# Batch 0's split q and k go to DRAM in two portions from two queues, and maxima units run 7 ahead in place of 8

## The reference

```
x = x + attention(modulate(x, cond))     # 16 heads of 8, rotary, causal softmax, output projection
x = x + ffn(experts(x, cond))            # 2 shared + 8 routed experts (top 2), then 8 zones (top 3)
```

## Time and profile before

| | us |
|---|---|
| median of 3 runs (lowest to highest) | 197.34 (197.03 to 198.95) |
| the profiled execution | 197.56 |
| its span | 195.8 |
| around the span | 1.76 |

### The profile page before, as it was taken

One profiled execution on the slowest core, in us unless ns is written; L12 is line 12 of the kernel. 1 busy time (PEld: TensorE's weight loads), 2 busy tenths in 40 slices (PEclk: granted clock), 3 DMA queues, 4 the chain that ended last, 5 costly groups with the idle time before them and its releaser, 6 DMA issues.

```text
span 195.8 us, 3320 instructions
## 1 busy us (share of the span) xinstructions
PE 180.1 (92%) x1006; PEld 124.1 (63%) x1006; DVE 143.7 (73%) x459; ACT 137.9 (70%) x228; POOL 83.6 (43%) x97
## 2 busy tenths in 40 slices
PE   7897698999999999898999999999799989999992
PEld 3654364666656666664467685786467857788881
DVE  5589699889898989896167974679969657556642
ACT  4479255486867768698843874576778899899880
POOL 4517359343324546464620620202467950497000
PEclk9999999999999999999999999999999999999999
DMA  4927657767585769431110899000000000001001
GB/s 143 363 85 229 203 189 233 205 176 223 161 264 157 223 184 253 141 96 54 54 50 5 274 310 311 5 2 0 0 2 3 0 0 0 0 2 57 0 0 54
DMA packets 13985, 23.06 MB, mean 118 GB/s; under 512 B 2632, under 2 KB 3784, under 8 KB 13912
## 3 DMA queue, kind: packets, MB, share of 16 engines
q1 hardware_dynamic: 13392, 22.46, 37.1%
q10 hardware_dynamic: 576, 0.39, 0.6%
HBM read 17.42 MB, written 6.09 MB: 120 GB/s over the span
## 4 chain that ended last, share of the span: by engine, by line
PE 61%; DVE 15%; ACT 11%; issue 6%; DMA 3%; SPq 2%; POOL 1%; DVEq 0%; ACTq 0%; POOLq 0%
PE psum L1414 9%; PE psum L1291 8%; PE psum L1416 8%; PE psum L1415 8%; PE psum L1342 7%; PE psum L1322 5%; DVE psum L680 3%; DMA t_q_pad<-scratch 2%; PE psum L1235 2%; PE psum L1249 2%; PE psum L1181 2%; DVE t_raw L826 2%; PE psum L1325 2%; ACT t_q_pad L1044 1%; DVE t_raw L830 1%
## 5 line engine op out<-in xcount | busy, mean ns | idle before, releaser
L680 DVE CUSTOM_DVE_ANT_0 psum<-psum,t_causal 128x128 f32<-128x128 f32 (+3 forms) x128 | 59.3, 525 | 8.0 <-PE psum L1291 7.3
L992 ACT ACTIVATE t_probs<-psum 128x768 f32<-128x768 f32 (+1 forms) x48 | 41.0, 880 | 4.9 <-PE psum L1322 3.3
L1291 PE MATMUL psum<-t_stacked,t_q_pad 128*128 128x256 f32 (+2 forms) x128 | 37.3, 361 | 3.9 <-issue 1.7
L576 POOL TENSOR_SCALAR_AFFINE_SELECT t_probs<-t_probs 128x512 f32<-128x512 f32 x32 | 20.0, 636 | 31.6 <-ACT t_probs L992 28.4
L1291 PEld LDWEIGHTS psum<-t_stacked,t_q_pad 128*128 128x128 f32 x128 | 21.4, 188 | 18.8 <-DVE t_row_max L680 10.8
L844 DVE SCALAR_TENSOR_TENSOR t_q_pad<-psum,t_zw_all,t_q_pad 128x512 fp32r<-128x512 f32 x24 | 17.9, 749 | 11.7 <-ACT t_q_pad L1042 11.6
L1028 ACT ACTIVATE t_raw<-psum 128x512 f32<-128x512 f32 x24 | 14.3, 595 | 10.4 <-PE psum L1460 7.7
L1342 PE MATMUL psum<-t_probs,t_v_all 128*32 128x512 f32 (+3 forms) x256 | 20.5, 439 | 0.0
L612 POOL TENSOR_TENSOR t_q_pad<-t_raw,t_q_pad 128x512 fp32r<-128x512 f32 x8 | 10.3, 1288 | 20.1 <-ACT t_q_pad L1044 20.1
L1322 PE MATMUL psum<-t_q_mov,t_k_pad 128*128 128x512 f32 (+1 forms) x64 | 18.4, 373 | 0.2
L680 DVE DVE_READ_ACCUMULATOR2_ANT t_row_max<- 128x1 f32 x128 | 18.4, 144 | 0.0
(11 more groups left out here) (228 smaller groups left out, 389.8 us busy)
## 6 DMA issues: line engine op xcount, KB each, us to landing
t_stacked<-scratch SPq DMA_DIRECT2D x14, 256.0 KB, 3.6
t_probs<-in_L_ffn_Wa SPq DMA_DIRECT2D x2, 1024.0 KB, 8.3
t_q_pad<-scratch SPq DMA_DIRECT2D x28, 64.0 KB, 3.2
t_k_pad<-scratch SPq DMA_DIRECT2D x28, 64.0 KB, 2.2
scratch<-t_o_sb SPq DMA_DIRECT2D x7, 256.0 KB, 2.0
t_raw<-in_experts SPq DMA_DIRECT2D x7, 256.0 KB, 3.4
scratch<-t_dn_hi SPq DMA_DIRECT2D x4, 256.0 KB
scratch<-in_rest SPq DMA_DIRECT2D x2, 448.0 KB
```

Of the source, the lines that this page charges most:

```text
L576: last = G.affine_select(out=tri, in_=tri, compare_op=ALU.is_ge, fill=0.0, base=0, pattern=[[0, HG], [1, P]], channel_multiplier=-1)
L680: last = V.tensor_tensor_reduce(scores, scores, causal[:, S - width:S], 1.0, 3 * BIG, ALU.add, ALU.max, row_max[s][:, qb, j:j + 1])
L992: A.activation(probs[s][:, c, 2 * h2:2 * h2 + 2, 0:w], ST[:, slot_of("exp", n, u):slot_of("exp", n, u) + 2, 0:w], ACT.Exp, scale=float(1.0 ...
L1291: last = T.matmul(ring("max", n, u)[:, i * 2 * P:i * 2 * P + width], q_pad[s][:, j, qb * P:(qb + 1) * P], stacked[:, 2 * n + 1, 0:width], ...
```

## The change

Four edits, which come together:

1. `spill` takes a queue, a range of groups, and the semaphores to count on. Batch 0 is written in two portions: group 1's 32 rows (64 KB for each DMA) and groups 2 and 3's 64 rows (128 KB).
2. The first portion of q and k stays where the spill was, on SP. Of the second portion, q goes on SP behind `pad_k(0)`, and k on ScalarE's own queue, between `copy_v(0)` and `copy_projection(1)`.
3. `ld_stack[n]` becomes a pair: M(n,0) waits for k's stack alone, the lay step for q's. The list of SP is reordered to match; the two parameter loads go behind `pad_k(1)`.
4. LEAD is 7: stage 0 holds 16 units (still 12 before the lay step), and in the stages n >= 1 each M unit sits one place later: places 0 to 4 are M(n+1,7..11), 5 to 11 are M(n+2,0..6).

```diff
-LEAD, FIRST = 8, 3
+LEAD, FIRST = 7, 3
...
+        spilled_1 = [sem(f"spilled_1{x}") for x in "qk"]
         spilled = [sem(f"spilled_{x}") for x in "qk"]
-        ld_stack = {n: sem(f"ld_stack{n}") for n in range(BY_PE, GROUPS)}
+        ld_stack = {n: [sem(f"ld_stack{x}{n}") for x in "qk"] for n in range(BY_PE, GROUPS)}
...
+        def spill(queue, first, last, i, done):
+
+            b = first // NG
+            q = slice(32 * (first - b * NG), 32 * (last - b * NG))
+            blocks = laid_blocks(first, last, i)
+            queue.wait_ge(hi_ready, 4 * b + (i + 1 if b else 3 + i))
+            for r in ((1, 2), (1, 3))[i]:
+                queue.dma_start(blocks[r], f32_of(qk_hi[q, i, :])).then_inc(done[i], 16)
+            queue.wait_ge(lo_ready, 4 * b + (i + 1 if b else 3 + i))
+            queue.dma_start(blocks[(3, 2)[i]], f32_of(qk_lo[q, i, :])).then_inc(done[i], 16)
...
             spill_rest()
-            spill(0, 0)
-            spill(0, 1)
+            spill(sp, 1, 2, 0, spilled_1)
+            spill(sp, 1, 2, 1, spilled_1)
             sp.wait_ge(rest_rows, 16 * 2)
-            sp.wait_ge(spilled[0], 16 * SPILLS)
+            sp.wait_ge(spilled_1[0], 16 * SPILLS)
             sp.wait_ge(pad1_zero, 1)
             pad_q(1)
-            sp.wait_ge(spilled[1], 16 * SPILLS)
-            load_stacked(1)
+            sp.wait_ge(spilled_1[1], 16 * SPILLS)
+            load_stacked_part(1, 1)
             sp.wait_ge(pads_zero, 1)
             pad_k(0)
-            load_stacked(2)
+            spill(sp, 2, NG, 0, spilled)
+            load_stacked_part(1, 0)
+            sp.wait_ge(spilled[1], 16 * SPILLS)
+            load_stacked_part(2, 1)
+            sp.wait_ge(spilled[0], 16 * SPILLS)
             pad_q(2)
+            load_stacked_part(2, 0)
+            sp.wait_ge(pads_zero, 2)
+            pad_k(1)
             sp.dma_start(small[:], io["small"]).then_inc(ld_small, 16)
             sp.dma_start(gate_rows[:], io["sel_e"]).then_inc(ld_sele, 16)
-            sp.wait_ge(pads_zero, 2)
-            pad_k(1)
...
             copy_v(0)
+            spill(act, 2, NG, 1, spilled)
             copy_projection(1)
...
                     pe.wait_ge(q_padded[s], 16 * HG * ((n + 1) // 2))
-                    pe.wait_ge(ld_stack[n], 16 * 2)
+                    pe.wait_ge(ld_stack[n][1], 16)
...
                     pe.wait_ge(rep_copied, 4)
+                else:
+                    pe.wait_ge(ld_stack[n][0], 16)
                 bank = ring("lay", n)
```

More of the change, by code:

```diff
@@ L354, in laid, with laid_blocks @@
             return scratch[GROUPS + 1 + i * (GROUPS - BY_PE) + n - BY_PE]
[L356 to L360, removed]
+        def laid_blocks(first, last, i):
+            at = GROUPS + 1 + i * (GROUPS - BY_PE) - BY_PE
+            return scratch[at + first:at + last].rearrange("g (j r d) t -> r (g j) d t", j=HG, r=KB)
+        def spill(queue, first, last, i, done):
[7 more added lines that the diff above has]
+            queue.dma_start(blocks[(3, 2)[i]], f32_of(qk_lo[q, i, :])).then_inc(done[i], 16)
         def slot_of(*item):
@@ L403, in pad_k @@
                     sp.dma_start(f32_of(k_pad[s][q, j, :]), src).then_inc(k_padded[s], 16)
[L405 to L412, removed]
             def spill_rest():
                 for i in range(2):
-                    first = GROUPS + 1 + i * (GROUPS - BY_PE)
-                    slots = scratch[first:first + GROUPS - BY_PE]
-                    rows = slots.rearrange("g (j r d) t -> r (g j) d t", j=HG, r=KB)[0]
+                    rows = laid_blocks(BY_PE, GROUPS, i)[0]
                     sp.dma_start(rows, io["rest"][i].unsqueeze(0).broadcast_to(
@@ L428, in load_stacked_part @@
             def load_stacked_part(n, i):
-                sp.dma_start(f32_of(stacked[:, 2 * n + i, :]), laid(n, i)).then_inc(ld_stack[n], 16)
+                sp.dma_start(f32_of(stacked[:, 2 * n + i, :]), laid(n, i)).then_inc(ld_stack[n][i], 16)
             def store_sums(n):
@@ L494, in _ @@
                 if n == 0:
-                    spill(1, 0)
+                    spill(sp, NG, GROUPS, 0, spilled)
                 if n + 2 < GROUPS:
@@ L498, in _ @@
                 if n == 0:
-                    spill(1, 1)
+                    spill(sp, NG, GROUPS, 1, spilled)
                 if n == NG:
```

## The result

| | before | after |
|---|---|---|
| median, us (lowest to highest, 20 runs each) | 197.41 (196.81 to 199.84) | 196.27 (195.28 to 198.88) |
| ratio, 95% interval | | 0.9922 (0.9897 to 0.9947) |
| profiled execution | 197.56 | 195.3 |
| its span | 195.8 | 193.5 |

The change saves 0.8%: clear of no change, but within the 1% that the prediction took for its limit. The forecast was 194.5, a gain of 3.1 us; the medians show 1.14. Single executions of one kernel differ by several us, and all ratios leave out those more than 1.5% above the kernel's fastest. The profiled execution of after is the second quickest of its 20, so the profiles show 2.26 us.

A forecast was written before the change was run, and what follows sets the result against it. The prediction took TensorE's 1.71 us hole before M(1,0), ended by a landing, then VectorE, then TensorE with small waits as the bound. It summed 197.56 - 1.5 (stage 0) - 1.6 (LEAD) to 194.5, range 193.2 to 196.9.

The forecast's parts named there:

- Waiting for k's stack alone: Ahead of M(1,0): without any other edit TensorE could start at 22.9, so 1.2 us are gained.
- T = 19.3: The time SP issues k's stack of group 1, taken between bounds of 17.6 and 20.3.
- project(1) as the new start: k's stack lands at 21.9, so TensorE goes on when project(1) ends at 22.47; the whole 1.71 us is gained.
- T stays at 20.3: First rival: the first portion lands no sooner, SP issues group 1's k stack at 20.3; 195.4 with LEAD, chance 0.15.
- pad_k(0)* follows: In stage 0 k_pad[0] lands at 23.8, before E(0,0) wants it at 24.33: nothing late.
- (at T = 20.3: 0.4): If SP issues k's stack of group 1 at 20.3, pad_k(0) is 0.4 us late for E(0,0).
- The signs of being wrong: M(1,0) starting after 23.5, group 1's lay step after 34, or lay steps 3 to 4 not below 8.97 - 0.1 apart.
- q_pad(2): Queued on SP behind q's second portion, it is issued near 27 and lands at 31.3; M(2,0) waits 1.7 us.
- The charge of 0.2: Stage 0: q_pad(2) puts group 1's lay step at 33.1 against 32.95, charged as 0.2 us.
- place_max escaping GpSimd: Stage 0, a bound only: 0.95 us more if VectorE's place_max also escapes GpSimd's operation.
- LEAD = 7: M(2,7) before E(1,0) -0.4, M(n+2,3) in stages 1 to 3 -0.84, q_pad(7)'s wait in stages 4 and 5 -0.34; together -1.6.
- LEAD gives nothing: Rival: the small waits only change places, with VectorE idle behind v's products; 196.1 us, chance 0.17.

The follow-up runs named there:

- e4: The changed kernel with ScalarE's three DMAs of k's second portion moved behind the lay copy; one execution, 198.94 us.
- e5: The changed kernel with k_pad[0] filled by four GpSimd copies in place of SP's four DMAs; 195.76 us, ratio 0.9909.
- e11: e8 with one added wait of GpSimd for place_max of group 1; 194.19 us, ratio 0.9816.
- e2: The changed kernel with LEAD taken back to 8; 197.51 us, ratio 0.9996.
- e0: The changed kernel, unedited; 196.03 us, ratio 0.9914.
- e8: e6 again: the kernel before with LEAD = 7, M(1,0) waiting for k's stack alone and k_pad(0) by GpSimd copies; 194.8 us, ratio 0.985.
- e9: e8 with LEAD taken back to 8; 196.45 us, ratio 0.9929.
- e1: The kernel before with LEAD = 7 and nothing else; 195.78 us, ratio 0.9918.
- e7: The changed kernel with LEAD = 6; 200.74 us, ratio 1.0183.
- e10: The kernel before with LEAD = 7 and M(1,0) waiting for k's stack alone, pad_k(0) still by DMA; 197.85 us, ratio 1.0011.
- e6: The kernel before with LEAD = 7, M(1,0) waiting for k's stack alone and k_pad(0) by GpSimd copies; 194.97 us, ratio 0.9886.
- e3: The changed kernel with k_pad[0] sent from ScalarE's queue and k's second portion from SP; 195.89 us, ratio 0.9898.

## Why the prediction was half right

- **Waiting for k's stack alone**, **T = 19.3**, **project(1) as the new start**: right. T was 19.09, M(1,0) started at 22.60 with nothing ahead of it. It was close: k's stack took 3.4 us to land in place of the 2.6 priced, and came at 22.5, 0.1 before it was needed. The rule of the Trainium skill that I weighed ("DMA: Bandwidth & Descriptors", "Why a DMA increments its semaphore by 16 and not by 1") agrees with the spread: the share is 0.26 beside a four-block spill, where the earlier trace rows has 0.71 and 1.01. What did not follow is that T stays at 20.3. From the first spill to the issue of k's stack it is 5.97 us in place of 7.49. Half of the 1.52 is in the issues, which cost 0.58 to 0.67 each in place of 0.79, so that the last went out 3.24 behind the first in place of 4.00. The other half is in its landing, 2.7 in place of 3.5.
- **The failed step** is "*pad_k(0)* follows: last issue T + 0.45 + 3 x 0.63, landing 2.1 later ... Nothing late." The issue time was right (21.4), the landing was 4.3 and not 2.1, and E(0,0) waited 1.45 of the 1.71 that had been gained. The 2.1 was a sound reading: the last piece of before, asked for alone, did land after 2.1. But a landing belongs to the traffic of its moment. The change itself put three writes of 128 KB from ScalarE's queue beside these reads. I priced them for ScalarE (free, and so they were) and never for the reads next to them. e4 takes them away, and the last piece lands after 2.6. The gain was bounded even without them: in before the last piece came at 23.1 + 2.1 = 25.2, so with the spills undivided and this landing E(0,0) could move from 26.04 by 0.8 at most, whatever M(1,0) did. (The bracket "(at T = 20.3: 0.4)" is off: with M(1,0) only 1.2 earlier E(0,0) is wanted at 24.84, and the 24.75 of that sum would be in time.)
- **The signs of being wrong**: one of the three came, the lay step of group 1 behind 34 (34.40). M(1,0) and the distance of the lay steps of groups 3 and 4 (8.74) came out as forecast.
- **q_pad(2)**: issued 27.95 against 27.3 forecast, late but hidden, since everything ahead of it was late as well. e5 uncovered it at once (1.26). The charge of 0.2 stood for a case that did not come.
- **place_max escaping GpSimd** stayed a bound, rightly: 1.18 in before and after. e11 shows the 0.95 is there to be had.
- **LEAD = 7**: the mechanism was right, and the size too: 1.6 forecast, 1.5 to 1.9 by the medians (e2 against e0, e8 against e9, e1 against before). In the profiles it is 1.99 (34.40 to 80.03 against 34.66 to 82.28). By terms: M(2,7) and the first M(n+2,3) gave 0.69 from lay step 1 to 2 for 0.68 forecast, the next two stages 0.22 each for 0.28, and stages 4 and 5 gave 0.86 for 0.34, because the wait for q_pad(7) was gone from that execution. It isn't gone from all: e1 has 0.42 of it. The rival "LEAD gives nothing" is refuted by e1. Its argument, that VectorE's idle time behind v's products would bring a wait back, is true one place further on (e7).
- **The sum**: stage 0 forecast -1.5, measured -0.26 to -0.57 in the profile and nothing by e2's median; LEAD -1.6, measured about that. (By the median the forecast is 194.2 and not 194.3.) That 196.27 lies within the range owes something to luck: the upper end was set for LEAD without effect, whose 196.1 is close to the measured time, and what happened is the opposite case, LEAD with its full effect and stage 0 with next to none. The profiled execution came out at 195.3, and its median 1 us above it; before, the profiled one lay 0.15 above its median of 20. Part of that distance is the clock: seven of the 20 runs of after have a mean granted clock of 0.983 to 0.989, and they are the ones at 196.49 to 198.88, with 197.12 the only other run above 196.33. It is not new with the change: 15 of the 63 runs of before in the three sets have 0.991 or less. How much of it the new hole of 1.45 us causes is not shown.

## What to carry to other kernels

When a wait goes, price the next one by the largest landing that the rows show for its kind, and not by the one that the last piece happened to have: here the same last piece took 2.1, 2.6, 3.4 and 4.3 to 4.8 us in different surroundings. Ask what the change itself sends beside it: transfers that nobody waits for can lengthen one that somebody does. A small copy that gates TensorE can be better made by an idle engine than by DMAs issued among writes (here 2.62 us for four, with no landing). Test each half of a compound change alone: here one half was the whole gain, and the other cost time once its bottleneck was removed.

## What the runs showed of the hardware that I had not expected

- The same four DMAs of 64 KB from SBUF to SBUF landed after 2.9/3.0/4.3 us beside three writes of 128 KB from another queue, and after 2.0/2.3/2.6 without them (e4, one execution); sending them from that other queue changed nothing (3.0/3.2/4.3).
- TensorE's granted clock went to its lower level of 1.2 GHz for about 3.5 us behind an idle stretch of 1.78 (e2) and 1.82 us (e10), and for over 6 us from within one of 3.81 (e4). The length of the stretch does not decide it alone: in their profiles it stayed full behind 1.45 (after), 1.71 (before) and 1.92 us (e7, whose 28 to 30 us read as below, where e2 and e10 have 0.50).

```profile
28.00:30.00 2.00, 1.93 (x10) 1.50 (x10) 2.00 (x8) 1.56 (x3) 1.44 (x2) 1.00 0.44 113
```

| kernel | longest idle stretch of TensorE from 20 to 32 us, in the profile | executions with a mean clock of 0.991 or less |
|---|---|---|
| e6, e8, e9, e11 | 0.33 to 0.67 | 0 of 30 |
| e1, e3, e5 | 1.07 to 1.26 | 6 of 30 |
| after and e0 | 1.39 to 1.45 | 8 of 26 |
| before | 1.71 | 15 of 63 |
| e2 | 1.78 | 5 of 12 |
| e10 | 1.82 | 11 of 12 |
| e7 | 1.92 | 4 of 6 |

So the lower clock comes more often with the longer stretches, and a stretch can cost more than its length: by their ratios e10 is 0.93% or 1.8 us slower than e1, with 0.75 us more in its longest hole. That the stretch is what brings it is argued from this table and not shown; no run varies it alone.

- VectorE's 128x16 operation takes 0.23 us alone. Beside a GpSimd operation on 128x512 that has begun before it, it lasts until just behind that operation's end (e8: 32.67 against 32.59; e7: 62.72 against 62.62), and a wait on GpSimd removes this. The Trainium skill says so ("SBUF — State Buffer", section "SBUF: two separate sides") for a VectorE operation with two inputs in SBUF and a GpSimd operation that reads SBUF, as these are: they take a shared pair of ports for a whole instruction, and the second to start is blocked until the first ends. The traces agree to within 0.1 us, and e11, in which VectorE's comes first, with 0.23. In e7 VectorE's operation with one input in SBUF (L698) is drawn out as well, to 62.11 against 62.04; whether it is of the other kind that the section names, one that uses two ports, the trace doesn't show.
